# Rebuilding the head of a two-stage sequence kernel: order of loads, conditioning in column quarters, fp32 for the first chunk

## The chip, the cores and the metric

One core of a Trainium2 chip. The metric is the device time of one execution in microseconds; three runs of the kernel before gave 1782.56 to 1783.31, median 1783.12. The profile is one further execution of the same kernel.

## The reference

There are 16 sequences x(b) of 512 tokens by 512 features. For each sequence b:

```
e     = [sin, cos](5000 * t[b] * freqs)                    # 128 values
m     = silu(e @ W1 + b1) @ W2 + b2                        # 512 values
scale = m @ Wsc + bsc ;  shift = m @ Wsh + bsh             # 512 values each
h     = silu(scale * norm(x, gamma, beta) + shift) @ W_in + b_in
x2    = silu(scale * norm(h, gamma, beta) + shift) @ W_out + b_out + x
o     = gelu(x2 @ Wi[e_b] + bi[e_b]) @ Wo[e_b] + bo[e_b] + x2
y     = row_norm(o) * g[e_b] + be[e_b]
```

`norm` takes mean and variance over the whole 512 x 512 sequence; `row_norm` over the features of a token. e_b is the expert of sequence b, one of 8, with a hidden size of 2048.

## The kernel before

Features lie on partitions, in 4 chunks (DC) of 128; the 512 tokens are columns. A precise product is made of three one-pass matmuls of fp32r parts, hi·hi, lo·hi and hi·lo (`three`, L445; all are recorded at L448). ScalarE makes the high parts (`copy`, L545), VectorE the low parts by subtraction (`lo_part`, L696).

**Steady state.** The expert layers run over 256 ticks k, 16 per sequence, one hidden tile of 128 each. In a tick TensorE makes `up(k)` (12 matmuls into hid_ps) and `down(k-2)` (12 into out_acc). The work of the next sequence's first stage (block A) is hung into these ticks by a table: STAGE_AT gives for each stage the tick at which the engines do it, STAGE_AT_1 (L77) the same for sequence 1, which follows the head. W_IN and W_OUT are the ticks at which TensorE makes one of four tiles of the two layers (`block_tile`, L468; 12 matmuls each). In each tick VectorE does in this order: low part of the gelu result (k-1), low parts of the expert weights (k+1 and k), residual additions, statistics, `totals`, `centre`, `affine`, low parts of h, then the 32x32 transposes of x2 (`turn`, 16 instructions a sequence, at ticks 2 to 5 by TURN_AT) and the final row norm. Each engine runs its list strictly in the written order; semaphores are waited for in that order too.

**The head** does for sequence 0 what has no steady state to hide it. SyncE issues the loads in the order head columns, W1, W2, x(0) by chunks, then scale/shift weights (`cond_w`), gamma/beta (`affine`) and W_in by chunks, W_out, the expert numbers and x(1); they land in about that order. TensorE multiplies zeros (`keep_warm`, L398) where it would wait. W1 and the encoding give m1 (L414), W2 gives m2 (`group`, L389), then each chunk's scale and shift (L434 to L443), all plain fp32 with the weights as the stationary operand and 16 (W1) or 112 columns, most of them padding, as the moving one; ScalarE adds the biases while it copies from PSUM (`cond_part`, L560). Mean and variance over partitions come from a product with a matrix of 1/128 (`average_of`, L403), `first_mean`, `first_var` on VectorE and a power on GpSimd. For each chunk c: `centre`, `affine` (VectorE), `silu`, `h_hi_part` (ScalarE), `h_lo_part` (VectorE), then 12 products, one for each output tile m and part (`first_block`, L458). ScalarE adds b_in and copies the result to `work` (`a_evac`, L619), the second norm reads `work`, the second layer follows in the same way, VectorE adds b_out and x (`x2_evac`, L773) and the first `up` starts.

## Time and profile before

| | |
|---|---|
| profiled execution | 1783.09 us |
| its span | 1781.3 us |
| TensorE busy | 1769.4 us, 99% |
| VectorE, ScalarE, GpSimd busy | 1286.1, 981.6, 101.6 us |
| first expert product starts | 51.31 us |
| last TensorE work starts | 1771.97 us |

The span is the time from the first to the last instruction in the profile. A matmul's row lasts longer than the distance to the next one, because matmuls overlap in the array: the distance of two starts is the cost of one. An fp32 matmul has two records, an fp32r one has one; both are written f32 in the rows.

### The profile page before, as it was taken

To read this page: it belongs to the slowest core of one execution; us is meant where nothing else is said; L and a number is where in the kernel's file an instruction comes from. 1 tells how busy PE (TensorE), PEld (TensorE's weight loads), DVE (VectorE), ACT (ScalarE), POOL (GpSimd) and SP (SyncE) were. 2 spreads that over 40 slices of the span, in tenths; PEclk is the share of its full clock that TensorE was granted. 3 is DMA by queue.
4 is the path that set the end of the run, shared out by engine and by line. 5 is a ranking of instruction groups with operands and counts; after the bars stand their busy time and mean duration, and the time that the engine had idled before them with its cause. 6 is when DMAs were issued, how large, how long until landed. Compare 5 with 4: busy or idle time off the path is not lost.

```text
span 1781.3 us, 22068 instructions
## 1 busy us (share of the span) xinstructions
PE 1769.4 (99%) x7834; PEld 1464.6 (82%) x7834; DVE 1286.1 (72%) x2136; ACT 981.6 (55%) x1562; POOL 101.6 (6%) x193
## 2 busy tenths in 40 slices
PE   9999999999999999999999999999999999999998
PEld 8788888888888888888888888888888888888886
DVE  6956777777777677777777677677777767767566
ACT  5656455565545656456564555645556554565442
POOL 0000000000000000000000000000000000000000
PEclk9999999999999999999999999999999999999999
DMA  7132331433323233332333313333143332322321
GB/s 290 55 129 74 122 110 57 137 108 98 109 90 138 75 107 107 115 110 71 122 109 98 111 70 122 111 121 110 57 144 103 98 110 99 130 74 89 116 95 59
DMA packets 45614, 189.33 MB, mean 106 GB/s; under 512 B 7042, under 2 KB 7042, under 8 KB 29122
## 3 DMA queue, kind: packets, MB, share of 16 engines
q1 hardware_dynamic: 43106, 183.96, 29.2%
q0 software_dynamic: 2400, 3.97, 2.1%
q8 instruction: 63, 1.03, 0.2%
q14 instruction: 45, 0.37, 0.1%
HBM read 171.10 MB, written 16.81 MB: 105 GB/s over the span
## 4 chain that ended last, share of the span: by engine, by line
PE 98%; DVE 1%; issue 0%; ACT 0%; POOL 0%; POOLq 0%; DVEq 0%; ACTq 0%
PE out_acc L448 39%; PE hid_ps L448 39%; PE blk_ps L448 18%; PE blk_ps L392 0%; PE hid_ps L401 0%; PE hid_ps L392 0%; POOL rstd_r L1012 0%; PE blk_ps L401 0%; DVE bn L710 0%; ACT work L610 0%; DVE bn_r L829 0%; DVE r_sb L824 0%; DVE x L778 0%; ACT h_hi L545 0%; DVE x_lo L696 0%
## 5 line engine op out<-in xcount | busy, mean ns | idle before, releaser
L448 PE MATMUL hid_ps<-x_hi,wi_hi 128*128 128x512 f32 x1024 | 398.9, 390 | 0.5 <-DVE x_lo L696 0.5
L448 PE MATMUL hid_ps<-x_hi,wi_lo 128*128 128x512 f32 x1024 | 398.4, 389 | 0.0
L448 PE MATMUL hid_ps<-x_lo,wi_hi 128*128 128x512 f32 x1024 | 398.4, 389 | 0.0
L448 PE MATMUL out_acc<-wo_hi,g_hi 128*128 128x512 f32 x1016 | 395.2, 389 | 0.0
L448 PE MATMUL out_acc<-wo_lo,g_hi 128*128 128x512 f32 x1016 | 395.2, 389 | 0.0
L448 PE MATMUL out_acc<-wo_hi,g_lo 128*128 128x512 f32 x1016 | 395.2, 389 | 0.0
L598 ACT ACTIVATE g_sb<-hid_ps,bi_sb 128x512 f32<-128x512 f32 x256 | 176.0, 688 | 317.0 <-PE hid_ps L448 316.6
L696 DVE TENSOR_TENSOR g_lo<-g_sb,g_hi 128x512 fp32r<-128x512 f32 x254 | 173.7, 684 | 195.7 <-ACT g_hi L602 194.0
L545 ACT ACTIVATE wo_hi<-stage 128x512 fp32r<-128x512 f32 x254 | 160.7, 633 | 173.1 <-PE out_acc L448 173.1
L448 PEld LDWEIGHTS hid_ps<-x_hi,wi_hi 128*128 128x128 f32 x1024 | 192.3, 188 | 42.2 <-DVE x_lo L696 1.7
L696 DVE TENSOR_TENSOR wo_lo<-stage,wo_hi 128x512 fp32r<-128x512 f32 x254 | 174.9, 689 | 69.6 <-ACT wo_hi L545 66.0
L448 PEld LDWEIGHTS hid_ps<-x_hi,wi_lo 128*128 128x128 f32 x1024 | 192.2, 188 | 40.0
L448 PEld LDWEIGHTS hid_ps<-x_lo,wi_hi 128*128 128x128 f32 x1024 | 192.1, 188 | 39.6
L448 PEld LDWEIGHTS out_acc<-wo_lo,g_hi 128*128 128x128 f32 x1016 | 190.8, 188 | 39.8
L448 PEld LDWEIGHTS out_acc<-wo_hi,g_hi 128*128 128x128 f32 x1016 | 190.6, 188 | 39.6
L448 PEld LDWEIGHTS out_acc<-wo_hi,g_lo 128*128 128x128 f32 x1016 | 190.7, 188 | 39.4
L448 PE MATMUL blk_ps<-h_hi,w_hi 128*128 128x512 f32 x480 | 186.8, 389 | 0.0
L448 PE MATMUL blk_ps<-h_lo,w_hi 128*128 128x512 f32 x480 | 186.7, 389 | 0.0
L448 PE MATMUL blk_ps<-h_hi,w_lo 128*128 128x512 f32 x480 | 186.7, 389 | 0.0
L798 DVE STREAM_TRANSPOSE x_turned<-x 32x512 f32<-32x512 f32 x256 | 179.6, 702 | 7.5
L696 DVE TENSOR_TENSOR wi_lo<-stage,wi_hi 128x512 fp32r<-128x512 f32 x256 | 174.8, 683 | 0.0
L602 ACT ACTIVATE g_hi<-hid_ps,bi_sb 128x512 fp32r<-128x512 f32 x254 | 173.3, 682 | 0.0
(102 smaller groups left out, 1688.4 us busy)
## 6 DMA issues: line engine op xcount, KB each, us to landing
stage<-in_expert_w SPq DMA_DIRECT2D x128, 1024.0 KB, 4.8
x<-in_xT SPq DMA_DIRECT2D x15, 1024.0 KB, 7.3
out_y<-r_sb SPq DMA_DIRECT2D x15, 1024.0 KB, 5.3
rows<-in_expert_rows SPq DMA_DIRECT2D x16, 512.0 KB, 6.7
mv_all<-mv_dram POOLq DMA_DIRECT2D x30, 128.0 KB, 3.9
stage<-in_cond_w SPq DMA_DIRECT2D x4, 512.0 KB, 9.2
affine_sb<-in_affine SPq DMA_DIRECT2D x4, 512.0 KB, 11.6
stage<-in_W SPq DMA_DIRECT2D x1, 1024.0 KB, 5.9
```

What stands on the lines that cost most here:

```text
L448: last = pe.matmul(dst, w[wp], xs[xp], start=start and i == 0, stop=stop and i == 2)
L545: return act.activation(out, in_, ACT.Copy)
L598: act.activation(g_sb[:, k % 2, :], hid_ps[k % 2][:, :], ACT.Gelu, bias=bi_sb[:, b % 2, i:i + 1]).then_inc(s_gelu, 1)
L602: act.activation(g_hi_of(k), hid_ps[k % 2][:, :], ACT.Gelu, bias=bi_sb[:, b % 2, i:i + 1]).then_inc(s_ghi, 1)
L696: return dve.tensor_tensor(out, full, hi.bitcast(F32), ALU.subtract)
L798: dve.transpose(dst[:, :, :, h, :], src[:, :, :, s, :]).then_inc(s_turn, 1)
```

## The change

Loads: x(0) comes right after W1, in two halves, then W2 in two halves, then for each chunk the norm weights, scale/shift weights and W_in; the host lays x, W2, W_out and the scale/shift weights out so that each partition reads one long run. A row of 2048 bias values (b2, bsc/bsh, b_in) goes to one partition of x(1)'s buffer, and x(1) itself is loaded only when the first layer is done.

Conditioning: the operands are swapped. The stationary operand is the batch (32 columns, 16 padded), the moving one the weights, in four strips j, each into 32 partitions of PSUM (`strips`), 128 columns wide for W1 and W2 and 64 for a chunk of scale and shift. Biases enter as products with a row of ones (K=1). The result is turned back by one VectorE 32x32-block transpose each (m1_raw, m2, `cond_turn`). b_in enters PSUM by four K=1 products of 512 columns (`b_in_products`).

Chunk 0 of both layers is one fp32 matmul per output tile from the raw weights and `work`, with no high and low parts (`first_products`). The second norm of sequence 0 reads the first layer's PSUM banks, `a_evac(0)` is gone, and the second layer goes to the other four banks. GpSimd makes two low parts of W_out. Statistics of x(1) move to tick 1, all stages of sequence 1 to later ticks; TURN_AT is unchanged. Low parts of chunk 0 of W_in and W_out, needed only from sequence 1 on, are made after the head.

```diff
-STAGE_AT_1 = STAGE_AT | {X_STATS: (), X_TOTALS: (1,), X_CENTRE: (1,), X_AFFINE: (2,),
-                         X_SILU: (3,), X_SPLIT: (4,), W_IN: (5, 5, 6, 6), A_TOTALS: (8,)}
+STAGE_AT_1 = STAGE_AT | {X_STATS: (), X_TOTALS: (4,), X_CENTRE: (4,), X_AFFINE: (5,),
+                         X_SILU: (5,), X_SPLIT: (6,), W_IN: (7, 7, 8, 8), A_TOTALS: (10,),
+                         A_CENTRE: (10,), A_AFFINE: (11,), A_SILU: (11,), A_SPLIT: (12,),
+                         W_OUT: (13, 13, 14, 14)}
+STATS_FIRST = 1
...
+def splits_before(turn):
+    return (DC - 1) * min(turn, 2) + DC * max(turn - 2, 0)
+def splits_of(b, which, c):
+    return splits_before(turn_of(b, which)) + (c if b == 0 else c + 1)
...
+        b2_row, bcond_row, bin_row = (x_sb[1][0:1, a:b, :].rearrange("p c n -> p (c n)")
+                                      for a, b in ((0, 1), (1, 3), (3, 4)))
+        ones = rows[0:1, 0, :]
...
-            return blk_ps[m % 2] if b else out_acc[m]
-        stat_bank = [out_acc[DC - 1], out_acc[0]]
+            if b:
+                return blk_ps[m % 2]
+            return cond_bank[m] if which else out_acc[m]
         cond_bank = hid_ps + blk_ps
+        stat_bank = [hid_ps[1], blk_ps[1]]
...
+            load(head_sb[:, :], head, ld_head)
+            load(w1_raw, W1, ld_w1)
+            load(x_sb[1][0:1, :, :].rearrange("p c n -> p (c n)"), bias_rows, ld_bias)
+            load_halves(x_sb[0], xT[0], ld_first)
+            load_halves(w2_raw, W2, ld_w2)
+            load(affine_sb[:, 0, 0, :], affine[0, :, 0:S], ld_affine[0])
             load_cond(0)
-            load_layer(0)
...
-            load_whole(x_sb[1], xT[1], ld_x[1])
+            load(affine_sb[:, 0, 1, :], affine[0, :, S:2 * S], ld_beta0)
+            load_w_in(0)
+            for c in range(1, DC):
+                load_affine(c)
+                load_cond(c)
+                load_w_in(c)
+                if c == 1:
+                    load(idx[:, :], itok.rearrange("(a b) -> a b", a=1), ld_idx)
+            load(w_raw[1][:, :, :].rearrange("p c n -> p (c n)"), W_out, ld_w_out)
...
-                        sp.wait_ge(s_mm2, 2)
+                        sp.wait_ge(s_mm2, 1)
+                    if b == 0 and j == 1:
+                        load_x(1)
...
-            def group(bank, n, w, src):
-                for c in range(DC):
-                    last = pe.matmul(bank[:, n * WIDE:(n + 1) * WIDE], w[:, c, :], src[:, c, :],
-                                     start=(c == 0), stop=(c == DC - 1))
+            def strips(bank, src, w, width, start=False, stop=False):
+                for j in range(P // BLOCK):
+                    last = pe.matmul(bank[BLOCK * j:BLOCK * (j + 1), 0:width], src, w(j),
+                                     start=start, stop=stop)
...
+            def of_w(w):
+                split = w.rearrange("p (c j q) -> p j c q", j=P // BLOCK, q=BLOCK)
+                return lambda j: split[:, j]
+            def of_cond(w):
+                return lambda j: w[:, j * 2 * BLOCK:(j + 1) * 2 * BLOCK]
+            def scale_shift(c):
+                bias = bcond_row[:, 2 * P * c:2 * P * (c + 1)]
+                strips(cond_bank[c], ones[:, 0:BLOCK], of_cond(bias), 2 * BLOCK, start=True)
+                pe.wait_ge(ld_cond[c], 16)
+                for k in range(DC):
+                    last = strips(cond_bank[c], m2[:, k, :], of_cond(cond_raw(c)[:, k, :]), 2 * BLOCK,
+                                  stop=(k == DC - 1))
+                last.then_inc(s_mmcond, 1)
+            def b_in_products(m):
+                pe.matmul(out_acc[m][:, :], bin_row[:, m * P:(m + 1) * P], ones, start=True, stop=False)
...
-            keep_warm(hid_ps[0], 9)
+            keep_warm(hid_ps[0], 7)
             pe.wait_ge(ld_w1, 16)
+            pe.wait_ge(s_pad, 1)
             pe.wait_ge(s_sin, 1)
-            for m in range(DC):
...
-                    average_of(0, 0, mv[:, 0, 0:1])
+            strips(blk_ps[0], enc_sin[:, :], of_w(w1_raw), P, start=True, stop=True).then_inc(s_mm1, 1)
+            keep_warm(hid_ps[0], 3)
+            pe.wait_ge(s_ones, 1)
+            pe.wait_ge(ld_bias, 16)
+            b_in_products(1)
+            pe.wait_ge(s_average, 1)
+            pe.wait_ge(s_mv, 1)
+            average_of(0, 0, mv[:, 0, 0:1])
+            keep_warm(hid_ps[0], 1)
             pe.wait_ge(s_sq, 1)
             average_of(0, 1, dev[:, 0, 1:2])
+            strips(blk_ps[1], ones[:, 0:BLOCK], of_w(b2_row), P, start=True)
             pe.wait_ge(s_pad, 2)
-            pe.wait_ge(s_m2, DC)
...
-                shift_of(m)
+            pe.wait_ge(s_m1, DC)
+            for k in range(DC):
+                if k % 2 == 0:
+                    pe.wait_ge(ld_w2[k // 2], 16)
+                last = strips(blk_ps[1], m1[:, k, :], of_w(w2_raw[:, k, :]), P, stop=(k == DC - 1))
+            last.then_inc(s_mm2, 1)
+            b_in_products(0)
+            pe.wait_ge(s_m2, 1)
+            scale_shift(0)
+            for m in range(2, DC):
+                b_in_products(m)
...
+            def first_products(which, m, c):
+                cols = slice(m * P, (m + 1) * P)
+                bank = block_bank(0, which, m)[:, :]
+                start = which == 1 and c == 0
+                if c == 0:
                     if m == 0:
-                        pe.wait_ge(s_wlo[which], c + 1)
...
-                        last.then_inc(s_blk, 1)
+                        pe.wait_ge(ld_w_out if which else ld_w_in[0], 16)
+                        pe.wait_ge(s_silu, DC * which + 1)
+                    return pe.matmul(bank, w_raw[which][:, 0, cols], work[:, 0, :], start=start, stop=False)
+                stop = c == DC - 1
+                if m == 0:
+                    pe.wait_ge(s_hhi, splits_of(0, which, c))
+                    if which and c < DC - 1:
+                        pe.wait_ge(s_wlopool, c)
+                    else:
+                        pe.wait_ge(s_wlo[which], 1 if which else c)
+                pe.matmul(bank, w_hi[which][:, c, cols], h_hi[:, c, :], start=False, stop=False)
+                pe.matmul(bank, w_lo[which][:, c, cols], h_hi[:, c, :], start=False, stop=False)
+                if m == 0:
+                    pe.wait_ge(s_hlo, splits_of(0, which, c))
+                last = pe.matmul(bank, w_hi[which][:, c, cols], h_lo[:, c, :], start=False, stop=stop)
+                if stop:
+                    last.then_inc(s_blk, 1)
+                return last
...
-            first_block(0, 0, [(m, 0) for m in range(DC)])
...
-            keep_warm(blk_ps[1], 8)
+            for c in range(DC):
+                for m in range(DC):
+                    first_products(0, m, c)
+                    if m == 0 and c + 1 < DC:
+                        scale_shift(c + 1)
+            keep_warm(blk_ps[0], 4)
             pe.wait_ge(s_mv, turn_of(0, 1) + 1)
             average_of(1, 0, mv[:, 1, 0:1])
-            keep_warm(blk_ps[1], 4)
+            keep_warm(blk_ps[0], 3)
             pe.wait_ge(s_sq, 2)
             average_of(1, 1, dev[:, 1, 1:2])
-            keep_warm(blk_ps[1], 16)
-            first_block(0, 1, [(m, c) for c in range(DC // 2) for m in range(DC)] +
-                        [(m, c) for m in range(DC) for c in range(DC // 2, DC)])
+            keep_warm(blk_ps[0], 10)
+            for c in range(DC // 2):
+                for m in range(DC):
+                    first_products(1, m, c)
+            for m in range(DC):
+                for c in range(DC // 2, DC):
+                    first_products(1, m, c)
...
-            for c in range(DC):
+            silu(0, 0, 0)
+            for c in range(1, DC):
                 w_hi_part(0, c)
-                scale_shift(c)
-                norm_end(0, 0, [c])
-            for c in range(DC // 2):
+                silu(0, 0, c)
+                h_hi_part(0, 0, c)
+            for c in range(1, DC):
                 w_hi_part(1, c)
-            for m in range(DC):
-                a_evac(0, m)
-            for c in range(DC // 2, DC):
-                w_hi_part(1, c)
+            w_hi_part(0, 0)
+            w_hi_part(1, 0)
             for k in range(FIRST_PAIR):
                 wi_hi_part(k)
                 wo_hi_part(k)
-            norm_end(0, 1)
+            silu(0, 1, 0)
+            for c in range(1, DC):
+                silu(0, 1, c)
+                h_hi_part(0, 1, c)
...
+                if (b, which) == (0, 1):
+                    src = block_bank(0, 0, m)[:, :]
+                else:
+                    src = (work if which else x_sb[b % 2])[:, m, :]
...
+            def cond_turn(c):
+                dve.wait_ge(s_mmcond, c + 1)
+                dve.transpose(cond_sb[:, c].rearrange("p k r -> p (k r)"), cond_bank[c][:, 0:2 * BLOCK]) \
+                   .then_inc(s_cond, 1)
+            dve.wait_ge(s_mm1, 1)
+            dve.transpose(m1_raw[:, :, :].rearrange("p c r -> p (c r)"), blk_ps[0][:, 0:P]).then_inc(s_m1turn, 1)
             for m in range(DC):
+            first_var(0)
+            dve.wait_ge(s_mm2, 1)
+            dve.transpose(m2[:, :, :].rearrange("p c r -> p (c r)"), blk_ps[1][:, 0:P]).then_inc(s_m2, 1)
             centre(0, 0, 0)
-            first_var(0)
...
-            w_lo_part(1, 1)
+            cond_turn(0)
+            affine(0, 0, 0)
+            centre(0, 0, 1)
+            affine(0, 0, 1)
+            cond_turn(1)
+            w_lo_part(0, 1, 1)
+            centre(0, 0, 2)
+            h_lo_part(0, 0, 1)
+            affine(0, 0, 2)
+            cond_turn(2)
+            w_lo_part(0, 2, 2)
+            centre(0, 0, 3)
+            h_lo_part(0, 0, 2)
+            affine(0, 0, 3)
+            cond_turn(3)
+            w_lo_part(0, 3, 3)
+            h_lo_part(0, 0, 3)
             for m in range(DC):
                 stats(0, 1, m)
...
             affine(0, 1, 0)
             affine(0, 1, 1)
             centre(0, 1, 2)
-            h_lo_part(0, 1, 0)
             affine(0, 1, 2)
             h_lo_part(0, 1, 1)
-            w_lo_part(1, 2)
             centre(0, 1, 3)
+            h_lo_part(0, 1, 2)
             affine(0, 1, 3)
-            h_lo_part(0, 1, 2)
-            w_lo_part(1, 3)
+            w_lo_part(1, 3, 6)
             h_lo_part(0, 1, 3)
             wi_lo_part(0)
-            for m in range(DC):
-                stats(1, 0, m)
+            wi_lo_part(1)
             for m in range(DC):
                 x2_evac(0, m)
                 if m >= 1:
                     x2_lo_part(0, m - 1)
             x2_lo_part(0, DC - 1)
-            wi_lo_part(1)
             wo_lo_part(0)
             wo_lo_part(1)
+            w_lo_part(1, 0, 8)
+            w_lo_part(0, 0, 8)
             for k in ticks:
...
+                if k == STATS_FIRST:
+                    for m in range(DC):
+                        stats(1, 0, m)
...
+            for c in range(1, DC - 1):
+                pool.wait_ge(s_whi, DC - 1 + c)
+                pool.tensor_tensor(w_lo[1][:, c, :], w_raw[1][:, c, :], w_hi[1][:, c, :].bitcast(F32),
+                                   ALU.subtract).then_inc(s_wlopool, 1)
```

## Rows read from the trace of the kernel before

**Rows 1.** The page: the chain that ended last, shares by engine.

```profile
PE 98%; DVE 1%; issue 0%; ACT 0%; POOL 0%; POOLq 0%; DVEq 0%; ACTq 0%
```

**Rows 2.** List of waits, TensorE, whole span: total us, times, longest.

```profile
PE out_acc L448 <- DVE h_lo L696: 0.6, 1, 0.6
PE hid_ps L448 <- DVE x_lo L696: 0.5, 2, 0.3
```

**Rows 3.** Timeline of TensorE: start us, us, engine, line, tiles, count, idle before.

```profile
1.31 4.21 PE L401 MATMUL hid_ps<-x_hi 128*128 128x512 f32 x9 [1.31 <-POOL x_hi L1022]
5.31 1.72 PE L414 MATMUL blk_ps<-enc_sin,g_sb 128*128 128x16 f32 x8
...
14.15 3.80 PE L392 MATMUL hid_ps<-m,stage 128*128 128x112 f32 x32 [0.45 <-issue]
17.79 1.95 PE L392 MATMUL blk_ps<-m,stage 128*128 128x112 f32 x16
19.51 0.48 PE L448 MATMUL out_acc<-h_hi,w_hi 128*128 128x512 f32 x1
...
32.07 0.39 PE L448 MATMUL out_acc<-h_hi,w_lo 128*128 128x512 f32 x1
...
40.19 0.47 PE L448 MATMUL out_acc<-h_hi,w_hi 128*128 128x512 f32 x1 [0.63 <-DVE h_lo L696]
...
55.34 0.39 PE L448 MATMUL hid_ps<-x_hi,wi_hi 128*128 128x512 f32 x1
...
60.78 0.39 PE L448 MATMUL out_acc<-wo_hi,g_hi 128*128 128x512 f32 x1
```

**Rows 4.** Timeline of TensorE's weight loads.

```profile
12.20 0.30 PEld L406 LDWEIGHTS out_acc<-mv,average 128*128 128x128 f32 x2
12.43 0.97 PEld L392 LDWEIGHTS blk_ps<-m,stage 128*128 128x128 f32 x8
```

**Rows 5.** The page: DMA issues, count, KB, us from issue to landing.

```profile
stage<-in_W SPq DMA_DIRECT2D x1, 1024.0 KB, 5.9
```

**Rows 6.** Busy time by stretch; last three columns granted clock, DMA share, GB/s.

```profile
0.00:10.00 10.00, 8.69 (x27) 7.34 (x27) 3.52 (x13) 3.75 (x8) 1.42 (x7) 1.00 0.81 275
10.00:20.00 10.00, 9.55 (x83) 9.46 (x83) 6.38 (x14) 4.49 (x13) 0.56 (x1) 1.00 1.03 407
```

**Rows 7.** Timeline of VectorE in the head.

```profile
8.28 2.69 DVE L710 BATCH_NORM_STATS2 bn<-x 128x6 f32<-128x512 f32 x4 [3.95 <-DMA x<-in_xT]
...
33.95 0.26 DVE L713 BATCH_NORM_AGGREGATE mv<-bn 128x2 f32<-128x24 f32 x1
...
46.42 2.46 DVE L710 BATCH_NORM_STATS2 bn<-x 128x6 f32<-128x512 f32 x4
...
53.01 1.47 DVE L696 TENSOR_TENSOR x_lo<-x,x_hi 128x512 fp32r<-128x512 f32 x2
```

**Rows 8.** Timeline of ScalarE in the head.

```profile
30.46 2.73 ACT L622 ACTIVATE work<-out_acc,head_sb 128x512 f32<-128x512 f32 x4 [1.42 <-PE out_acc L448]
...
37.78 0.82 ACT L610 ACTIVATE work<-work,shift_sb,scale_sb 128x512 f32<-128x512 f32 x1 [1.48 <-DVE work L765]
```

**Rows 9.** Timeline of GpSimd.

```profile
0.73 0.53 POOL L1022 MEMSET x_hi<- 128x512 f32 x1 [0.29 <-POOLq L1079]
```

**Rows 10.** Timeline of VectorE in ticks 1 to 4.

```profile
58.02 0.28 DVE L720 BATCH_NORM_STATS2 mean_bn<-mv_all 128x6 f32<-128x128 f32 x1
...
58.62 2.74 DVE L755 SCALAR_TENSOR_TENSOR work<-x,mean_all,affine_sb 128x512 f32<-128x512 f32 x4
61.28 0.69 DVE L696 TENSOR_TENSOR g_lo<-g_sb,g_hi 128x512 fp32r<-128x512 f32 x1
...
63.08 2.74 DVE L765 SCALAR_TENSOR_TENSOR work<-work,rstd,affine_sb 128x512 f32<-128x512 f32 x4
...
68.23 3.64 DVE L798 STREAM_TRANSPOSE x_turned<-x 32x512 f32<-32x512 f32 x5
...
73.72 2.49 DVE L696 TENSOR_TENSOR h_lo<-work,h_hi 128x512 fp32r<-128x512 f32 x4
```

More of the change, by code:

```diff
@@ L55 @@
 EPS_B = 1e-12
-B1, B2, BSC, BSH, BIN, BOUT = (i * DC for i in range(6))
+B1, BIN, BOUT = (i * DC for i in range(3))
 TURN_1 = 6.28125
@@ L116, in const_columns, with build @@
     return np.stack([np.concatenate([freq, freq]), turns, radians], axis=1).astype(np.float32)
-def build(nc, xT, itok, head, W1, W2, cond_w, affine, W_in, W_out,
+def build(nc, xT, itok, head, W1, W2, cond_w, bias_rows, affine, W_in, W_out,
           expert_w, expert_bi, expert_rows, mv_dram, y):
@@ L210, in build @@
         blk_ps = [ps(f"blk_ps{n}") for n in range(2)]
-        ld_head, ld_idx, ld_w1, ld_w2 = (sem(f"ld_{n}") for n in ("head", "idx", "w1", "w2"))
+        ld_head, ld_idx, ld_w1, ld_bias = (sem(f"ld_{n}") for n in ("head", "idx", "w1", "bias"))
+        ld_w2 = [sem("ld_w2a"), sem("ld_w2b")]
+        ld_beta0 = sem("ld_beta0")
         ld_cond = [sem(f"ld_cond{m}") for m in range(DC)]
-        ld_first = [sem(f"ld_first{c}") for c in range(DC)]
+        ld_first = [sem("ld_first_a"), sem("ld_first_b")]
         ld_affine = [sem(f"ld_affine{c}") for c in range(DC)]
@@ L313, in _, with load, load_halves @@
-            load_cond(1)
-            load_cond(2)
-            load_layer(1)
-            load_cond(3)
-            load_layer(2)
-            load_layer(3)
-            load_whole(w_raw[1], W_out, ld_w_out)
-            sp.dma_start(idx[:, :], itok.rearrange("(a b) -> a b", a=1)).then_inc(ld_idx, 16)
-            load_whole(x_sb[1], xT[1], ld_x[1])
+            def load(dst, src, done):
+                sp.dma_start(dst, src).then_inc(done, 16)
+            def load_halves(dst, src, done):
+                half = DC // 2
+                for h in range(2):
+                    load(dst[:, h * half:(h + 1) * half, :].rearrange("p c n -> p (c n)"),
+                         src[:, h * half * D:(h + 1) * half * D], done[h])
@@ new lines, in load_cond, with load_affine, load_w_in @@
+            def load_cond(c):
+                load(cond_raw(c).rearrange("p c n -> p (c n)"), cond_w[c], ld_cond[c])
+            def load_affine(c):
+                load(affine_sb[:, c].rearrange("p a n -> p (a n)"), affine[c], ld_affine[c])
+            def load_w_in(c):
+                load(w_raw[0][:, c, :], W_in[c * P:(c + 1) * P, :], ld_w_in[c])
+            load(head_sb[:, :], head, ld_head)
+            load(w1_raw, W1, ld_w1)
+            load(x_sb[1][0:1, :, :].rearrange("p c n -> p (c n)"), bias_rows, ld_bias)
@@ L762, in affine @@
                 at = work[:, c, :]
+                if (b, which, c) == (0, 0, 0):
+                    dve.wait_ge(ld_beta0, 16)
                 dve.wait_ge(s_stat, turn_of(b, which) + 1)
@@ L1059, in columns, with chunks @@
         return v.reshape(-1, P).T
+    def chunks(w):
+        return w.reshape(DC, P, D).transpose(1, 0, 2).reshape(P, DC * D)
     arrays = {
[L1062 removed]
+        "xT": a["x"].transpose(0, 2, 1).reshape(B, DC, P, S).transpose(0, 2, 1, 3).reshape(B, P, DC * S),
         "itok": a["itok_B_0_7"],
         "head": np.concatenate([np.broadcast_to(a["condB_t"], (P, B)), const_columns()] +
[L1065 to L1069 removed]
+                               [columns(A[n]) for n in ("b1", "b_in", "b_out")], axis=1),
+        "W1": A["W1"], "W2": chunks(A["W2"]),
+        "cond_w": np.stack([A["Wsc"], A["Wsh"]]).reshape(2, DC, P, DC, P // BLOCK, BLOCK)
+                    .transpose(3, 2, 1, 4, 0, 5).reshape(DC, P, 2 * DC * P),
+        "bias_rows": np.concatenate([A["b2"], np.stack([A["bsc"], A["bsh"]])
+                                     .reshape(2, DC, P // BLOCK, BLOCK).transpose(1, 2, 0, 3).reshape(-1),
+                                     A["b_in"]]).reshape(1, -1),
         "affine": np.stack([A["gamma"].T, A["beta"].T]).reshape(2, DC, P, S).transpose(1, 2, 0, 3)
                     .reshape(DC, P, 2 * S),
[L1072 removed]
+        "W_in": A["W_in"], "W_out": chunks(A["W_out"]),
         "expert_w": pack_experts(E["Wi"], E["Wo"]),
```

149 lines of the change are left out of this document (44 added, 105 removed).

## The prediction

> **What bounds the kernel now.** I read the chain of waits first: 98% of it is TensorE, nearly all in L448, the split products [rows 1]. The list of waits then says that TensorE loses only about a microsecond to others: 0.6 us before the second layer of sequence 0, and two short ones before the first expert product [rows 2]. The timeline of TensorE shows the same in order of time: a head, a ragged first expert product, and from 55.34 a stream without a gap: 24 matmuls of 512 columns to 60.78, 5.44 us, 0.227 each [rows 3]. The change leaves the work of that stream as it is. So the time is: when does the product that started at 55.34 start now, and does the stream stay closed.
>
> The profiled execution took 1783.09 us, its span 1781.3, with 1.8 around it; it is the middle one of the runs (median 1783.12), so differences are added to 1783.1.
>
> I split the head at B, the end of the last product of layer one: 32.07 + 0.39 = 32.46 [rows 3].
>
> **What the small fp32 matmuls cost.** An fp32 matmul is two records. With 112 columns 32 records take 14.15 to 17.79, 0.114 each; with 16 columns 8 records last 1.72 us from 5.31, about 0.2 each, at half rate: the nine 512-column ones from 1.31 to 5.31 are 0.444 apart against 0.227 later, so that stretch ran at the lower level of 1.2 GHz, although its granted clock reads 1.00 [rows 3, 6]. Weight loads of the one-column product stand 12.20 to 12.43 for two, 0.115 each [rows 4]. Seven times fewer columns gives no shorter record: the weight load of 128 columns sets about 0.11, not the streaming. A 512-column product of one pass takes 0.227, so two passes over 128 columns are 0.107-0.114, over 64 columns 0.057, and over 512 columns two records make 4 x 0.22 = 0.88 a matmul.
>
> The new head has 104 quarter matmuls, 208 records: W1 8, b2 and W2 40, and each of the four scale/shift chunks 40. The trace has no matmul into a quarter of the partitions. Bounds for 40 records: if weight loads stay at 0.108 and nothing overlaps, 4.3 us for any; if the load shrinks with the 32 columns but streams are serial, 4.4 (W2, 128 columns) and 2.3 (64 columns); if the second record of one quarter runs beside the first of the next, half of that, 2.25 and 1.15; if all four quarters stream at once, 1.1 and 0.6. I take the halves: both records of one matmul use the same quarter, so they follow each other, and only neighbours can overlap. Before, a chunk of scale/shift was 16 records, 17.79 to 19.51, 1.72 us [rows 3].
>
> The Trainium skill (TensorE: Matmul & The Clock Gate, Part 3: Packing small matmuls) says that matmuls in different column quarters start some 4 ns apart and run side by side, in order. By it all four might stream at once, 1.1 and 0.6 us; no row here shows it. It is a rival below, with its time from the bounds just given.
>
> **Up to B.** DMA: head, W1 and x(0) are now the first 1.33 MB, the same bytes that head, W1 and W2 were; W2 landed 5.9 after its issue at 1.66, at 7.6, so x(0) lands there and its first half near 6.2 [rows 5]. W2 ends at 2.38 MB, where x(0) ended, near 10.2. Chunk 0 of scale/shift follows at about 12.1 at the 407 GB/s of the second window, gain, offset and W_in(0) by 13.4 [rows 6]; the chunks after that total the same bytes as before and come before they are needed. The bias rows are 8 KB; later x(1) and stage loads have cover until 53 and 30.
> W1's quarters end about 6.2; DVE transposes 128 elements a partition (no row; below, 0.26 of the 24-element aggregate, above, 0.69 of the 512-element transposes; taken 0.28, DVE's row of 128 elements [rows 7, 10]) and takes statistics, 2.69 + 0.3 as before [rows 7]: 9.5 instead of 11.26. With the distances that the second norm had when TensorE was free (33.95 to 37.00), mean at 10.0, squares 10.4, variance and rstd 12.0. On TensorE b_in(1) (K=1, 0.88 at full rate) sits in the wait. b2 and W2: 10.6 to 12.9. Transpose to m2 13.4, beside b_in(0), to 13.8. Scale/shift chunk 0: 15.0. Now a chain that was ACT only: transpose 15.4 (DVE), affine 16.1, silu 0.85 [rows 8], 17.0; b_in(2) and b_in(3), 1.76, fill TensorE's wait. First product at 17.05 against 19.51. The chunk-0 products are 4 x 0.88 = 3.5 instead of 12 x 0.227 = 2.7, chunks 1 to 3 are 8.2, three scale/shift groups 3.5, small h_lo waits 0.2, drain 0.2: B = 32.65, 0.2 later than before. What is won in front is spent in twice the records (208 for 104) and in fp32.
>
> **From B to the first dense expert product.** Statistics now read PSUM (ACT's four evacuations cost 0.68 each like its SBUF work; DVE's four from SBUF 2.69; I take no difference, bounds 0 and 0.1 each, and only the last comes after B): variances at B + 1.03 instead of 33.95 + 0.26 = B + 1.75; those evacuations [rows 8] are gone. From there to the end of silu(0), 34.21 to 38.60, 4.4 us [rows 7, 8], unchanged; then fp32 takes it without high and low part: B + 5.5 against 40.19 = B + 7.7. Its chunk costs 0.8 more. The second layer (its last low part is ready at B + 11.9, in time) then ends at B + 17.4, before at 40.19 + 48 x 0.23 = B + 18.9: 1.5 won. The DVE statistics of x(1), 2.46 + 0.3 at 46.42, stood before the residual additions and held them back; now they are in tick 1. So the last low part of x ends 2.05 after the block instead of 3.0: Z = B + 19.45 (before 54.4, the end of the row at 53.01 [rows 7]), and the stream starts at Z + 0.94 = B + 20.4 against B + 22.9. Won: 2.5 us. POOL's two low parts of W_out have no row; the nearest is its 128x512 memset, 0.53 [rows 9], taken as the lower end; the upper is five times that, an estimate. They have cover from about B - 3, when ACT has the high parts, to B + 2.5, when the second rstd is due, 2.7 each, and cost nothing in either case; beyond it the excess would delay that rstd.
>
> **The stall that comes later.** Stages of sequence 1 move two ticks back, but the 16 transposes of sequence 0 stay in ticks 2 to 5. Count DVE from Z [rows 10]: three low parts of a tick 1.8, centre 2.66, affine 2.65, five transposes 3.67, totals 0.6, first h_lo 0.62. After Z: four low parts of weights 2.5 (two W_out/W_in chunk 0 are new there), tick 1 low parts 1.2, statistics 2.7; tick 2: 1.8 + 0.7; tick 3: 1.8 + 3.7; tick 4: 1.8 + 0.6 + 2.7 + 3.7; tick 5: 1.8 + 2.7 + 3.7; tick 6: 1.8 + 0.6. Sum 33.8: the first h_lo of sequence 1 is ready at Z + 33.8. TensorE reaches the block at tick 7: Z + 0.94 + 2.72 + 5 x 5.44 = Z + 30.9. It stands 3 us. Before, the same account closes: TensorE reached it at 55.34 + 2.72 + 3 x 5.44 = 74.4, and h_lo was ready at 73.72 + 0.63 = 74.35, with no wait in the list [rows 2, 3, 10]. Behind the waiting block stand up(7) and all of the stream, so it is all paid. ACT's late silu and its table changes end just under DVE's queue. Lower bound 0, if the account is as much too high somewhere; upper 3.7, if ACT adds 0.7. After tick 7, ticks with block tiles are 10.9 us and DVE catches up; at 13 and 14 two tiles stand in one tick, same work.
>
> Sum: B +0.2, to the stream -2.5, stall +3.1 (the 3 and a drain): +0.8. Forecast 1783.1 + 0.8 = 1783.9.
>
> **Rivals.** (1) Quarters all at once, and no stall. First product 15.3, three groups 1.8 instead of 3.5, so B = 28.9, -3.6; with -2.5: -6.1, 1777.0. For it: four separate quarters of output; against: two records per matmul on one quarter, and the DVE account. Only one of the two: all at once with stall 1780.1, no stall with halves 1780.8.
> (2) No overlap: the other side. Place: W1, W2 and four scale/shift groups on TensorE. statistics later by 0.7 through W1's serial records, W2 2.2, four groups 4 x 1.15: 7.4 more than the forecast, 1791.3. It decides, by over 0.2%, when a record of 64 columns costs over 0.04 (0.029 + 0.028 x 2.8 / 7.4). If the load doesn't shrink at all: 40 records 4.3, about 1800.
> (3) The wait before tick 7 leaves TensorE idle for 3 us, and the clock falls. The head shows what half rate costs: 0.444 instead of 0.227, from 1.31 over the records of 5.31, and back at 0.115 by 12.20 [rows 3, 4], so 4 to 10.9 us. Taken 8.8, it costs 4.4: 1788.3. Against: the idle stretch is short. The Trainium skill (the same page, HAM oscillation — how this bites in real kernels) says that an idle gap between bursts halves the clock; the longest idle of TensorE after its start is 0.6 here, so no row bears on it.
>
> **Chances.** Forecast 0.30; all at once without stall 0.24; no stall with halves 0.10; all at once with stall 0.07; no overlap 0.17; loads not shrinking 0.05; clock 0.07. About 0.2% (3.6 us) is what a measurement tells from no change. Faster: 0.24. Same: 0.28 + 0.17 = 0.45. Slower: 0.02 + 0.29 = 0.31. The range holds down to 1777 and up to 1792, leaving out the dearest loads and the tail of (1); the likeliest case's own is 1781 to 1787.
>
> **What would show it.** The spacing of quarter records: 0.03 (halves), 0.06 (serial), 0.11 (load bound). First product of layer one at 17, B at 32.7. The last statistics 1 us after B; second layer 5.5 after B. On TensorE one wait of about 3 us for h_lo, some 31 us after the first dense expert product, DVE busy without gap before it. No such wait, or quarters closer than 0.03, makes the forecast wrong on the fast side; quarters above 0.04 on the slow side.

## The result, and the profile after

The changed kernel takes 1790.48 us (median of 5 runs, 1789.64 to 1793.83), against 1782.56 (5 runs, 1782.46 to 1783.31) for the kernel before in the same comparison: ratio 1.0049, 95% interval 1.0034 to 1.0063. It is slower by 7.9 us, or 0.5%. The prediction was 1783.9, in a range of 1777 to 1792. The time lies inside the range, and on the side to which 0.31 was given. That it lies inside is luck: the likeliest case's own range ended at 1787, and what lies above it was there for quarters that don't overlap and for a clock that falls in tick 7. Neither is what made this profile longer.

The profiled execution took 1790.48 us, its span 1788.7, so the span is 7.4 longer than before. The chain of the page, with shares by engine, answers to [rows 1], and the list of TensorE's waits to [rows 2]:

```profile
PE 96%; DVE 2%; issue 1%; DMA 0%; ACT 0%; POOL 0%; SPq 0%; POOLq 0%; DVEq 0%; ACTq 0%
```

```profile
PE blk_ps L494 <- DVE h_lo L750: 3.3, 1, 3.3
PE hid_ps L436 <- DVE mv L772: 3.2, 1, 3.2
```

Two waits of some 3 us are new. One is for the first low part of the block of sequence 1 (tick 7), the stall that the prediction counted. The other stands in the head: TensorE waits for the mean and variance of x(0). The timeline of TensorE (start, us, engine, line, tiles, count, idle before) answers to [rows 3]:

```profile
10.84 0.56 PE L436 MATMUL hid_ps<-mv,average 128*128 128x1 f32 x2 [3.16 <-DVE mv L772]
...
12.99 1.94 PE L422 MATMUL blk_ps<-stage,m 128*32 128x128 f32 x32
...
17.23 1.08 PE L422 MATMUL hid_ps<-stage,m 128*32 128x64 f32 x32
18.24 3.78 PE L459 MATMUL out_acc<-rows,x 1*128 1x512 f32 x4
...
29.67 0.65 PE L422 MATMUL blk_ps<-stage,m 128*32 128x64 f32 x32
...
39.08 0.40 PE L525 MATMUL out_acc<-h_lo,w_hi 128*128 128x512 f32 x1
...
59.46 0.39 PE L494 MATMUL hid_ps<-x_hi,wi_hi 128*128 128x512 f32 x1
...
92.86 0.47 PE L494 MATMUL blk_ps<-h_hi,w_hi 128*128 128x512 f32 x1 [3.33 <-DVE h_lo L750]
```

Three rows divide the 7.4 us. Layer one now ends at B = 39.08 + 0.40 = 39.48, before at 32.46 [rows 3]: +7.0 (the prediction had +0.2). The dense expert stream starts at 59.46 = B + 20.0, before at 55.34 = B + 22.9: −2.9 (predicted −2.5). The late wait is +3.3 (predicted +3.1). 7.0 − 2.9 + 3.3 = 7.4, and nothing is left over. Two of the three terms came as written; the third is off by 6.8 us, and it is where layer one ends.

What happened there is in the windows of TensorE (stretch: length, busy, matmuls in brackets, then granted clock, DMA share, GB/s), which answer to [rows 6]:

```profile
8.00:10.00 2.00, 0.00 (x0) 0.89 0.99 372
10.00:12.00 2.00, 1.17 (x4) 0.50 1.01 303
...
24.00:26.00 2.00, 2.00 (x42) 0.50 1.04 419
26.00:28.00 2.00, 2.00 (x5) 0.84 1.03 417
28.00:30.00 2.00, 2.00 (x37) 1.00 0.99 414
```

The engine stands idle from 7.7 to 10.8, and within that wait the granted clock falls to 0.50, the level of 1.2 GHz. It stays there until some 26.6, though from 12.99 on TensorE is busy without a gap. The rows of the timeline say the same by their lengths. The four bias records at 18.24 (two fp32 matmuls of 512 columns) take 3.78; the like four of experiment e5 below, at full rate, take 1.98. The same 32 quarter records of 64 columns take 1.08 at 17.23 and 0.65 at 29.67. The wait itself is no loss against the prediction, which had it (the mean was due at 10.0 there): the loss is some 16 us of conditioning and layer one done at half rate.

### The profile page after: what moved, and what is told of

It is laid out like the page before. It is cut to its first block, busy times and chain, and to the rows that moved or that the text cites. A ratio compares the mean times of both kernels' runs of the same rounds, so it can differ in the third digit from the quotient of the medians.

```text
span 1788.7 us, 22235 instructions
## 1 busy us (share of the span) xinstructions
PE 1771.5 (99%) x7924; PEld 1455.0 (81%) x7924; DVE 1285.9 (72%) x2138; ACT 974.6 (54%) x1544; POOL 104.1 (6%) x196
## 4 chain that ended last, share of the span: by engine, by line
PE 96%; DVE 2%; issue 1%; DMA 0%; ACT 0%; POOL 0%; SPq 0%; POOLq 0%; DVEq 0%; ACTq 0%
PE hid_ps L494 38%; PE out_acc L494 38%; PE blk_ps L494 18%; DVE x_turned L862 1%; DMA x<-in_xT 0%; PE out_acc L459 0%; PE out_acc L513 0%; PE blk_ps L422 0%; DVE work L829 0%; DVE work L817 0%; DVE bn L769 0%; PE out_acc L521 0%; PE out_acc L525 0%; DVE wi_lo L750 0%; POOL rstd_r L1095 0%
```

## The experiments

The first theory (1) was that the idle stretch in the head costs the clock, and that the stretch needs only to be filled. The second (2) was that what follows it, matmuls of one row (`b_in_products`, K = 1) and into quarters (32 columns of the array), doesn't bring the clock back either, whatever is in front. The late wait was to be tested by itself. All the kernels e1 to e6 and e8 are the changed kernel with the edits shown; e7 is the kernel before with one. None leaves work out. Ratios are against the kernel before on the same chip (1782.93 for e1 to e4, 1782.86 for the others).

**e1, the wait filled.** Fifteen more products of zeros, on a bank whose sums they don't change:

```diff
             b_in_products(1)
+            keep_warm(hid_ps[0], 15)
             pe.wait_ge(s_average, 1)
```

> The changed kernel with one edit: 15 products of zeros (128x512, one pass) more on TensorE behind the first b_in product, in the 3.2 us in which it waits for the variances of x(0). Theory 1: that idle stretch (7.7 to 10.8) is what halves the clock, and the half rate then makes W2, b_in, scale/shift and the first chunk slow until 26.7. Then the granted clock stays 1.00 over the head, the first product of layer one starts near 17 instead of 21.8, layer one ends near 32 instead of 39.5, and the kernel is 7 to 8 us faster than the changed kernel, 1782 to 1784, level with the kernel before. Theory 2: products with one row (K=1) and products into a quarter do not hold the clock. Then it falls anyway, some microseconds after the quarter and one-row products begin at about 11.9, and the gain is 0 to 4 us (1786 to 1791). The late wait of 3.3 us for h_lo stays in both.

Measured: 1789.98 (1788.14 to 1792.21), ratio 1.0041 (1.0028 to 1.0055), span 1786.3. The profiled execution is the fastest of its five. By the device times the filling gained 0.5 us at the medians, and its interval overlaps that of the changed kernel (1.0034 to 1.0063): a gain is not shown there. What follows is read from the one profile. The wait in the head is gone, and the dense stream starts at 54.13, 5.3 earlier than in the changed kernel. But the clock holds only to 18, and falls with no idle time before it. TensorE's timeline and windows of e1:

```profile
17.14 1.10 PE L514 MATMUL out_acc<-work,r_sb 128*128 128x512 f32 x2
```

```profile
16.00:18.00 2.00, 1.90 (x5) 1.00 1.05 412
18.00:20.00 2.00, 2.00 (x42) 0.66 1.02 400
20.00:22.00 2.00, 2.00 (x3) 0.50 1.03 407
...
86.00:88.00 2.00, 0.45 (x1) 0.72 0.86 291
88.00:90.00 2.00, 2.00 (x6) 0.50 1.04 434
```

What stood ahead of the fall, with TensorE busy from 11.8 on, were b2, W2, `b_in` and two chunks of scale/shift, all of them one-row or quarter matmuls, and between them only the two whole-row records of 17.14. Theory 1 explains no fall there; theory 2 allows it, and e2 tests it. The clock also falls in the late wait, which in the changed kernel's profile it did not. Span: −1.2 to the stream (54.13 for 55.34), +3.3 late wait, and of the +5.0 against before 2.9 is left for half rate after that wait.

**e2, the wait filled and the `b_in` products made whole.** The same product with all 128 rows: the stationary operand has b_in in its first row and zeros below, the moving one ones. (The code cut leaves out two lines: GpSimd writes ones into all 128 rows, and SyncE issues the bias row and the loads behind it, x(0) among them, only after the memset.)

```diff
+            dve.memset(x_sb[1][:, 3, :], 0.0).then_inc(s_binz, 1)
...
-                pe.matmul(out_acc[m][:, :], bin_row[:, m * P:(m + 1) * P], ones, start=True, stop=False)
+                pe.matmul(out_acc[m][:, :], x_sb[1][:, 3, m * P:(m + 1) * P], rows[:, 0, :], start=True, stop=False)
```

> The edit before, and the four b_in products work with 128 rows (127 of them zero) in place of one; columns, passes and results are the same. Theory 1: no difference to the filled wait alone, the clock is held in both. Theory 2: the full-row products (0.88 us each at full rate) stand between the quarter products and hold the clock: the granted clock stays 1.00 to the first product of layer one, and this one is 3 to 8 us faster than the filled wait alone. If neither holds the clock, the quarter products alone are enough to lose it: 1786 to 1791.

Measured: 1786.39 (1783.86 to 1787.21), ratio 1.0016 (1.0007 to 1.0025), span 1785.2. The granted clock is 1.00 throughout the head; the stream starts at 53.34, 2.0 before that of the kernel before. The interval lies below that of e1, so the gain over e1 is shown by the device times too. The filling is longer than the wait, though: VectorE has the variances at 9.69, and TensorE, busy with zeros, comes to the mean at 11.25 (VectorE and TensorE of e2):

```profile
9.42 0.27 DVE L774 BATCH_NORM_AGGREGATE mv<-bn 128x2 f32<-128x24 f32 x1
```

```profile
11.25 0.28 PE L437 MATMUL hid_ps<-mv,average 128*128 128x1 f32 x2
```

With the filling TensorE comes to the mean 1.6 us after the variances here, 1.1 in e1, 1.0 in e4 and 0.2 in e5; without it, 0.15 (the changed kernel, e3, e6). What differs is when x(0) landed and when the first matmuls were done: the variances were there at 9.60 (e1, e3), 9.69, 9.73 (e4), 10.00 (e5), 10.06 (e6), 10.23 (e8) and 10.69 (the changed kernel), one profile each. Starts of the stream therefore compare to about 1 us only. What is left is the late wait and what it does to the clock (windows of TensorE in e2):

```profile
84.00:86.00 2.00, 0.00 (x0) 0.88 0.52 74
86.00:88.00 2.00, 1.25 (x3) 0.50 0.95 397
88.00:90.00 2.00, 2.00 (x6) 0.50 1.03 430
```

−2.0 and +3.3 make +1.3; the span is 3.9 longer, so half rate after the wait costs 2.6. That is the prediction's rival 3 at its own place, for 2.6 us where it had 4.4. The eleven runs of e2 go from 1783.86 at a mean clock of 0.999 to 1787.21 at 0.996, so the clock may fall after this wait in some executions and not in others; only the profiled run, at 0.996, shows it.

**e6, whole rows alone,** without the filling: does the fall in the idle stretch matter if what follows can end it?

> The changed kernel with only the full-row b_in products (128 rows, 127 of them zero); the 3.2 us wait for the variances stays open. Theory 1 (the idle wait drops the clock): it falls at about 10 as before, but now two, then four full products stand among the quarter products at 15 to 22, so the clock is back before 22 in place of 26.7: 2 to 4 us faster than the changed kernel, 1786.5 to 1788.5. Theory 2 (only the thin products matter): the clock holds, 4 us or more faster, 1786.4 or below, as with both edits.

Measured: 1787.74 (1786.11 to 1788.5), ratio 1.0026 (1.0015 to 1.0037), span 1786.1. The waits of TensorE and its windows:

```profile
PE hid_ps L437 <- DVE mv L773: 3.3, 1, 3.3
PE blk_ps L495 <- DVE h_lo L751: 3.3, 1, 3.3
```

```profile
10.00:12.00 2.00, 1.63 (x19) 0.90 1.00 341
12.00:14.00 2.00, 2.00 (x33) 0.50 1.04 413
14.00:16.00 2.00, 2.00 (x38) 0.74 1.02 415
```

The same wait is there and the clock falls after it, but it is back at about 15 instead of 26.6, and the stream starts at 53.97 instead of 59.46. Only the row count of the four bias products (and the order of the memset and the loads) differs. To leave out when x(0) landed and how long the filling was, I count from the product for the mean to the stream: 10.84 to 59.46 is 48.6 in the changed kernel, 10.21 to 53.97 is 43.8 in e6, 10.74 to 54.13 is 43.4 in e1, 11.25 to 53.34 is 42.1 in e2. So of 6.5 us between the changed kernel and e2, the short fall with whole rows behind it is 1.7, and the clock that doesn't come back is 4.9. Either edit takes most of it in these profiles, and they don't add. The device times agree for e6 (1.0026 against 1.0049, intervals that barely touch), but don't tell e6 from e2.

**e3, the late wait alone.** Head as changed; the transposes of the output of sequence 0, which stand in VectorE's queue ahead of sequence 1's stages, later:

```diff
 TURN_AT = {2: (0, 1), 3: (1, 6), 4: (6, 11), 5: (11, 16)}
+TURN_AT_0 = {2: (0, 1), 3: (1, 6), 4: (6, 8), 5: (8, 9), 6: (9, 12), 7: (12, 16)}
```

> The changed kernel with one edit: seven of the sixteen transposes of sequence 0 move behind the last low part of h (ticks 6 and 7 in place of 4 and 5). My account of VectorE says that its queue is 3.1 us late at the first block product of sequence 1 and that 7 x 0.73 = 5.1 us less work before it clears this. Then the wait of 3.3 us for h_lo is gone, nothing takes its place, and the kernel is 3.3 us faster than the changed kernel (1787). Rival: ScalarE, whose high parts come behind a late silu and two table changes, is next by under 1 us: 2.3 to 3 us are won. Rival: x(2), which waits for the transposes, and the expert weights queued behind it on SyncE come late: a new wait in ticks 9 to 11, nothing won.

Measured: 1787.59 (1786.36 to 1788.78), ratio 1.0025 (1.0015 to 1.0036), span 1785.7: 2.9 less than the changed kernel by the medians, 3.0 by the spans. Of the 3.0, 2.3 is the late wait, and 0.6 the stream's start, which the edit doesn't touch: the variances were there 1.1 earlier in this profile. TensorE's row at the end of the wait, before it in the changed kernel 3.33:

```profile
89.93 0.47 PE L495 MATMUL blk_ps<-h_hi,w_hi 128*128 128x512 f32 x1 [1.03 <-DVE h_lo L751]
```

The head stays slow: its wait for `mv` is 2.1 in this profile, the clock 0.50 from 10 to 26, the stream at 58.82. So the cause of the late wait is what the prediction said, the length of VectorE's queue, and it goes when that is shortened.

**e4, all three,** the edits of e2 and e3 together.

> All three edits: filled wait, full-row b_in products, transposes later. If they are independent: 7 to 8 us (clock) and 3.3 us (transposes) faster than the changed kernel, 1779 to 1780, which is 3 us faster than the kernel before. If the quarter products lose the clock by themselves: 1784 to 1787.

Measured: 1781.88 (1781.4 to 1783.54), ratio 0.9995 (0.9986 to 1.0004), span 1780.1. Stream at 52.84 (−2.5), late wait 1.3: −1.2, the whole difference of the spans. The interval holds 1: by the device times this kernel is not told from the kernel before. The rest of the late wait was no longer VectorE's load. VectorE itself stood, in its row just ahead of the stages, for ScalarE (VectorE and ScalarE of e4):

```profile
81.57 0.69 DVE L753 TENSOR_TENSOR g_lo<-g_sb,g_hi 128x512 fp32r<-128x512 f32 x1 [2.87 <-ACT g_hi L662]
```

```profile
76.01 2.94 ACT L670 ACTIVATE work<-work,cond_sb 128x512 f32<-128x512 f32 x4 [1.99 <-DVE work L832]
78.97 1.28 ACT L658 ACT_TABLE_LOAD   x1
```

ScalarE's silu waits for VectorE's affine, which stands behind the transposes; then VectorE waits for ScalarE's next high part, which stands behind the silu and a table load. To get the affine out earlier, more transposes have to leave ticks 3 to 5.

**e5, transposes later still:**

```diff
-TURN_AT_0 = {2: (0, 1), 3: (1, 6), 4: (6, 8), 5: (8, 9), 6: (9, 12), 7: (12, 16)}
+TURN_AT_0 = {2: (0, 1), 3: (1, 3), 4: (3, 4), 5: (4, 6), 6: (6, 11), 7: (11, 16)}
```

> The kernel with all three edits, and the transposes of sequence 0 further back: 6 by tick 5 in place of 9, so 3 fewer (2.2 us) stand ahead of the affine steps of sequence 1. In the kernel with all three edits TensorE still waits 1.3 us at the first block product of sequence 1, and there VectorE waits for ScalarE, whose silu began at 76.0 when the affine step arrived. Theory: the silu comes 2 us earlier, the wait of 1.3 us goes and nothing takes its place: 1780.6, and about 2.3 us less than the kernel before. Rival: ScalarE's two table changes around the silu set the end whatever comes before: no change, 1781.9.

Measured: 1781.12 (1780.66 to 1781.88, 11 runs), ratio 0.999 (0.9981 to 0.9999), span 1779.2. It is the fastest kernel here, 1.7 us under the kernel before by the medians; the interval just leaves out 1. Its timeline of TensorE, its row in the list of waits, and its windows:

```profile
11.66 1.08 PE L424 MATMUL blk_ps<-stage,m 128*32 128x128 f32 x32
...
13.97 0.65 PE L424 MATMUL hid_ps<-stage,m 128*32 128x64 f32 x32
14.56 1.98 PE L461 MATMUL out_acc<-rows,x 128*128 128x512 f32 x4
16.63 1.10 PE L516 MATMUL out_acc<-work,r_sb 128*128 128x512 f32 x2
...
32.21 0.39 PE L528 MATMUL out_acc<-h_lo,w_hi 128*128 128x512 f32 x1
...
52.90 0.40 PE L497 MATMUL hid_ps<-x_hi,wi_hi 128*128 128x512 f32 x1
```

```profile
PE blk_ps L497 <- DVE h_lo L753: 0.3, 1, 0.3
```

```profile
8.00:10.00 2.00, 2.00 (x11) 1.00 0.94 349
10.00:12.00 2.00, 1.84 (x27) 1.00 1.03 355
```

Stream −2.4, late wait +0.3, span −2.1.

**e7, the stage table alone.** The kernel before with the later stages of sequence 1 and the later statistics of x(1), and the old head:

```diff
-STAGE_AT_1 = STAGE_AT | {X_STATS: (), X_TOTALS: (1,), X_CENTRE: (1,), X_AFFINE: (2,),
-                         X_SILU: (3,), X_SPLIT: (4,), W_IN: (5, 5, 6, 6), A_TOTALS: (8,)}
+STAGE_AT_1 = STAGE_AT | {X_STATS: (), X_TOTALS: (4,), X_CENTRE: (4,), X_AFFINE: (5,),
+                         X_SILU: (5,), X_SPLIT: (6,), W_IN: (7, 7, 8, 8), A_TOTALS: (10,),
+                         A_CENTRE: (10,), A_AFFINE: (11,), A_SILU: (11,), A_SPLIT: (12,),
+                         W_OUT: (13, 13, 14, 14)}
+STATS_FIRST = 1
```

> The kernel before with one part of the change: the later ticks of sequence 1, and the statistics of x(1) in tick 1 instead of ahead of the residual additions. Nothing of the head's front is touched. Theory: the additions start as soon as their products end, so the dense stream starts 1.0 us earlier (54.3 instead of 55.3); then VectorE, with the 16 transposes in ticks 2 to 5 ahead of the block, is 2.3 us late at the first block product of sequence 1: 1.3 us slower in all, 1784.2, or some 2 us more where the clock falls in that wait. Rival: the late wait belongs to the new head (the two low parts behind it), then there is none here and the kernel is 1 us faster than before, 1781.9.

Measured: 1786.87 (1785.22 to 1787.43), ratio 1.0022 (1.0013 to 1.0031), span 1784.8. TensorE's timeline and windows:

```profile
87.39 0.47 PE L451 MATMUL blk_ps<-h_hi,w_hi 128*128 128x512 f32 x1 [3.28 <-DVE h_lo L699]
```

```profile
85.00:90.00 5.00, 2.61 (x8) 0.80 0.83 269
90.00:95.00 5.00, 5.00 (x21) 0.86 0.88 352
```

The wait is 3.3, 1.0 more than I had expected from it: the two low parts of weights that the new head adds to VectorE's queue (1.2 us) are not here, and it is as long all the same. The subtraction was wrong. One low part of Wi stands behind the residual additions here that the new head has ahead of them (0.6), and then VectorE waits for ScalarE:

```profile
56.05 0.69 DVE L699 TENSOR_TENSOR g_lo<-g_sb,g_hi 128x512 fp32r<-128x512 f32 x1 [0.46 <-ACT g_hi L605]
```

So VectorE comes to the low part of tick 1's gelu result 3.0 us after Z in both kernels (53.04 to 56.05, and 58.51 to 61.53). The stream starts at 53.98, −1.4; of this 0.4 is that layer one ended 0.4 earlier (31.66 + 0.39 = 32.05) with the head unchanged, and 0.9 the edit. −1.4 + 3.3 = 1.9 of a span that is 3.5 longer; 1.6 is left for the clock. This part of the change costs 4.0 us by itself, with the old head.

**e8, quarters in turn.** e4, with the products of W2 and of scale/shift ordered so that one quarter of the array is finished before the next begins; the same matmuls:

```diff
-            for k in range(DC):
-                if k % 2 == 0:
-                    pe.wait_ge(ld_w2[k // 2], 16)
-                last = strips(blk_ps[1], m1[:, k, :], of_w(w2_raw[:, k, :]), P, stop=(k == DC - 1))
+            for h in range(2):
+                pe.wait_ge(ld_w2[h], 16)
+            last = by_quarter(blk_ps[1], m1, lambda k: of_w(w2_raw[:, k, :]), P)
```

> The kernel with all three edits (1781.9), with W2's and scale/shift's quarter products in another order: all four of one quarter of PSUM, then the next quarter; the same products with the same results. If the four quarters stream side by side only because neighbours go to different quarters, as the trace says (four starts 7 ns apart, the next four 60 ns on at full rate, 64 columns), the order takes that away: a scale/shift group's 32 records go from 0.55 to about 1.8 us, W2's from 1.0 to 3.5, together 2.5 + 4 x 1.25 = 7.5 us more before the layers, 1787 to 1789. Rival: the engine overlaps them in any order, or the products are hidden behind other waits: 1782 to 1783.

Measured: 1785.91 (1785.35 to 1786.51), ratio 1.0016 (1.0007 to 1.0025), span 1784.3, 4.0 us slower than e4. Timeline of TensorE:

```profile
12.42 2.46 PE L431 MATMUL blk_ps<-stage,m 128*32 128x128 f32 x32
...
16.11 1.39 PE L431 MATMUL hid_ps<-stage,m 128*32 128x64 f32 x32
```

32 records of 64 columns now take 1.33 from start to start, 0.042 each, against some 0.58 and 0.018 in e5 (13.97 to 14.56). The order with neighbours in different quarters is worth some 4 us here. The 7.5 that I expected assumed 0.057 a record and no overlap at all. The 32 starts from 16.11 fall into four runs of eight. Within a run they are 0.056 apart (the first two 0.080), and each run begins 6 ns after the fifth start of the run before. So, if a run is a quarter, quarters run beside each other in this order too, for part of the time.

All the spans, as terms against the kernel before (us; "rest" is what the span has beyond the two terms, where the windows show the clock at half after the late wait):

```
                     stream starts   late wait   rest   span
changed kernel           +4.1          +3.3       0.0   +7.4
e1 fill                  -1.2          +3.3      +2.9   +5.0
e6 whole rows            -1.4          +3.3      +2.9   +4.8
e2 fill, whole rows      -2.0          +3.3      +2.6   +3.9
e7 stage table alone     -1.4          +3.3      +1.6   +3.5
e3 transposes later      +3.5          +1.0      -0.1   +4.4
e8 quarters in turn      +2.0          +1.0       0.0   +3.0
e4 all three             -2.5          +1.3       0.0   -1.2
e5 later still           -2.4          +0.3       0.0   -2.1
```

## Why the prediction came out as it did

**The spacing of quarter matmuls** (halves: 0.029 a record of 64 columns). Wrong: they are cheaper than that. All four quarters run at once: 0.018 a record, 32 in 0.65 [e5]. A whole group of 40 records, from 17.66 to 18.48 in e5, takes 0.82, between the 0.6 of rival 1 and the 1.15 taken. The starts of neighbours lie 7 ns apart in the trace. The Trainium skill (TensorE: Matmul & The Clock Gate, Part 3: Packing small matmuls) has some 4 ns and concurrent running; the trace agrees on the second, and has 7 for the first.

**x(0) in front and the conditioning up to the first product** (17.05). The order of the steps was right, and with the clock held the first product stands at 16.63. Two sizes were off by themselves. In this profile the halves of x(0) landed later than I took it: statistics began at 7.86 and ended 10.43, not at 9.2, and the variances were there at 10.69, not 9.5. In the other profiles of the same loads they were there from 9.60 on, so 9.5 was near the early end. Transposes of 128 elements took 0.32, not 0.28. VectorE's rows of the changed kernel, which answer to [rows 7]:

```profile
5.40 0.32 DVE L950 STREAM_TRANSPOSE m_raw<-blk_ps 128x128 f32<-128x128 f32 x1 [1.11 <-PE blk_ps L422]
...
7.86 2.53 DVE L769 BATCH_NORM_STATS2 bn<-x 128x6 f32<-128x512 f32 x4 [2.14 <-DMA x<-in_xT]
10.43 0.26 DVE L772 BATCH_NORM_AGGREGATE mv<-bn 128x2 f32<-128x24 f32 x1
```

**B = 32.65.** This is the step that failed. With the clock held its number is right to 0.1 in e5 (32.21 + 0.39 = 32.60) and in e4 (32.53), and to 0.4 in e2 (33.03), partly by luck: in e4 three groups of scale/shift took 2.5 in place of 3.5, and the products of chunks 1 to 3 9.6 in place of 8.6 with their waits and drain. In the changed kernel it is 39.48, because the prediction let `b_in(1)` sit in the wait and looked no further at what the wait was: 3 us of idle TensorE. It weighed an idle stretch against the clock for tick 7 alone, and gave it 0.07. Before, the longest idle stretch after the start was 0.6 us [rows 2], so nothing in the trace said what 3 us do, but the working itself had the idle stretch in the head: W1's quarters end at 6.2, one `b_in` product of 0.88 follows, the mean is due at 10.0. Behind a fall the size was unforeseen as well. I had 4 to 10.9 us of half rate from the start-up of the kernel before, where whole-row products of zeros run; here it lasted 17 us, 16 of them with TensorE busy. Whole rows in the four bias products ended it after some 3 us (e6 against the changed kernel). The Trainium skill (the same page, HAM oscillation — how this bites in real kernels) says that an idle gap between bursts halves the clock; the 3.2 us in the head agree, the late wait of 3.3 in the same profile doesn't.

**From B to the stream** (−2.5). Right: −2.9 in the changed kernel. In e5 it starts 52.90 − 32.60 = 20.3 after B, −2.6 where −2.5 was forecast. The parts came close too: in the changed kernel the second layer begins at 44.54, B + 5.1 (forecast 5.5), before at B + 7.7; and e7, with the moved statistics of x(1) alone, has 53.98 − 32.05 = 21.9 after B, −0.9, as forecast for them. GpSimd's two low parts took 1.28 each, inside the bounds, and nothing waited for them:

```profile
36.70 2.56 POOL L1113 TENSOR_TENSOR w_lo<-x_turned,w_hi 128x512 fp32r<-128x512 f32 x2 [23.30 <-ACT w_hi L615]
```

**The late stall** (+3.1, of VectorE's queue of 33.8 us). Right in place, cause and size: Z is 58.51 and the first low part is ready at 92.65, Z + 34.1. VectorE's idle time in between is 0.2. The same account missed e7 by 1.0 us, where a wait for ScalarE stood in for the work taken out. VectorE's rows in ticks 4 to 7 of the changed kernel, which answer to [rows 10], have the transposes in front of the centre, the affine and the low parts:

```profile
78.29 3.64 DVE L862 STREAM_TRANSPOSE x_turned<-x 32x512 f32<-32x512 f32 x5
...
83.78 2.73 DVE L829 SCALAR_TENSOR_TENSOR work<-work,rstd,affine_sb 128x512 f32<-128x512 f32 x4
86.54 3.65 DVE L862 STREAM_TRANSPOSE x_turned<-x 32x512 f32<-32x512 f32 x5
...
92.03 2.49 DVE L750 TENSOR_TENSOR h_lo<-work,h_hi 128x512 fp32r<-128x512 f32 x4
```

**The rivals.** All at once (1) is true of the quarters, and gave nothing visible in the changed kernel. Its 1777 needed no stall and a held clock: with both repaired, e5 is at 1781.1, since its first product stands at 16.63 and not at 15.3. (Its terms also give B = 29.2, 0.3 later than the 28.9 written.) No overlap (2) is false; that its 1791.3 lies nearest to the measured time is chance. The clock (3) is the true one, with its price right in kind, in the head for 7 us, and after the late wait only in e1, e2, e6 and e7, for 1.6 to 2.9. Why it doesn't fall in the changed kernel's own late wait is open: its window 90 to 95 reads 1.00 with a wait as long. So is the spread of its five runs, 4.2 us against 0.9 before: their mean granted clocks are 0.991 and 0.992 at 1793.2 and 1793.8, 0.994 at the profiled 1790.5 and at 1789.6, but 0.997 at 1790.3, which this account doesn't explain; only the profiled run has a trace.

## What to carry to other kernels

When an edit makes one step of the head ready sooner, ask what TensorE does until the next thing it needs: an idle stretch of 3 us cost 1.7 us here with whole-row products close behind it (e6 against e2), and 6.5 with one-row and quarter products (the changed kernel against e2), through the clock. Price such a wait together with what runs after it; where such a wait can't go, fill it with products of zeros, no more of them than the wait is long (with 15 TensorE came to the mean 1.0 to 1.6 us after the variances in e1, e2 and e4), and keep whole-row products close behind. And when stages are moved later in a queue, move what stands between them as well: counting the queue of one engine against the arrival of another gave the stall to 0.2 us here, and to 1.0 in e7, where a wait for a third engine was left out.

## What the runs showed of the hardware

- TensorE's granted clock fell without an idle stretch: in e1 between 18 and 20 us, with TensorE busy, nearly all of it one-row and quarter matmuls. With the four b_in products made whole rows and the quarter ones left as they are (e2) it stayed at 1.00. One profile each.
- An idle stretch of 3.2 to 3.3 us was followed by half rate in six of seven places (the head in the changed kernel and e6; the late wait in e1, e2, e6 and e7), and not in the seventh. The head's wait of 2.1 in e3 was followed by it too; late waits of 1.0 (e3, e8) and 1.3 (e4) were not.
- Fp32 matmuls into the four quarters of the array: 32 records of 64 columns 0.65 us at full rate and 1.08 at half; of 128 columns 1.08 and 1.94. Before, 32 records of 112 columns with the whole array took 3.64 from start to start [rows 3]. Ordered quarter by quarter the 64-column ones took 1.39, in four runs of eight starts 0.056 apart, each run beginning beside the last three records of the one before (e8).
- A one-row fp32 product of 512 columns costs what a 128-row one does: four records take 1.98 in e1 (one row) and 1.98 in e5 (128 rows).
